# Relative products and causal attention merged into one stage

## The reference

```
q = layernorm(x) @ Wq + bq ;  k = ctx @ Wk + bk ;  v = ctx @ Wv + bv       # per head: [512, 16]
QEr[i, r] = q[i] . Er[r]                                                   # Er: [512, 16]
Srel      = skew(QEr)               # Srel[i, j] = QEr[i, 511 - (i - j)] for j <= i
attn      = softmax((q k^T + Srel) / sqrt(16), causal)
out       = attn @ v
```

## Time and profile before

| | |
|---|---|
| median of three runs | 6249.43 us (6245.49 to 6275.58) |
| span of the profiled execution | 6247.0 us |
| instructions in it | 101,680 |
| PE, DVE, ACT, POOL busy over the span | 74%, 63%, 46%, 33% |
| mean granted TensorE clock | 0.858 of full speed |

### The profile page before, as it was taken

One profiled execution on the slowest core, in us unless ns is written; L12 is line 12 of the kernel. 1 busy time (PEld: TensorE's weight loads), 2 busy tenths in 40 slices (PEclk: granted clock), 3 DMA queues, 4 the chain that ended last, 5 costly groups with the idle time before them and its releaser, 6 DMA issues. The chain is left out here.

```text
span 6247.0 us, 101680 instructions
## 1 busy us (share of the span) xinstructions
PE 4641.5 (74%) x24902; PEld 2868.6 (46%) x24902; DVE 3907.9 (63%) x8145; ACT 2867.3 (46%) x6151; POOL 2042.9 (33%) x3122
## 2 busy tenths in 40 slices
PE   7455666493879973998676767797677887995897
PEld 4113333342643331885234645686555663333433
DVE  6344555538547875443678956558866556886565
ACT  2235655215227753223564556435456323773353
POOL 0113443000036630221443554124542214542342
PEclk9558989696988986999778989998889998997897
DMA  4999986100063321111551232002321115332533
GB/s 158 283 360 190 211 197 157 45 0 0 0 201 89 97 63 45 43 43 41 155 144 62 102 115 65 27 13 92 129 73 41 28 49 182 92 85 82 179 117 100
DMA packets 317791, 648.30 MB, mean 104 GB/s; under 512 B 73170, under 2 KB 128115, under 8 KB 317384
## 3 DMA queue, kind: packets, MB, share of 16 engines
q1 hardware_dynamic: 245912, 450.68, 22.7%
q0 software_dynamic: 71488, 193.32, 13.1%
HBM read 373.99 MB, written 238.70 MB: 98 GB/s over the span
## 5 line engine op out<-in xcount | busy, mean ns | idle before, releaser
L1115 DVE TENSOR_REDUCE t_nmax<-t_aps 128x2 f32<-128x1024 f32 x700 | 838.0, 1221 | 278.2 <-PE t_aps L1037 272.6
L1222 ACT ACTIVATE t_expT<-t_bps 128x512 f32<-128x512 f32 x1290 | 700.9, 599 | 284.4 <-PE t_bps L1056 235.4
L1056 PE MATMUL t_bps<-t_Q,t_K 51*128 51x512 f32 (+2 forms) x1290 | 525.9, 468 | 60.8 <-ACT t_expT L1222 43.8
L1037 PE MATMUL t_aps<-t_K,t_Q 49*128 49x512 f32 (+2 forms) x1400 | 464.7, 460 | 64.7 <-DMA t_K<-k_halves 28.9
L1056 PEld LDWEIGHTS t_bps<-t_Q,t_K 51*128 51x128 f32 (+2 forms) x1290 | 228.8, 189 | 528.6 <-ACT t_expT L1222 373.5
L2517 DVE TENSOR_TENSOR f_hl<-f_h,f_hh 128x512 fp32r<-128x512 f32 x192 | 203.7, 1061 | 413.3 <-ACT f_hh L2442 413.3
L1083 PE MATMUL t_ops<-t_expT,t_V 128*17 128x512 f32 (+1 forms) x2560 | 414.2, 614 | 0.5 <-ACT t_expT L1222 0.4
L3923 ACT ACTIVATE t_relsb<-t_relsb,t_nmax 128x128 f32<-128x128 f32 (+3 forms) x515 | 277.6, 559 | 272.8 <-DVE t_nmax L3896 264.0
L3857 PE MATMUL t_tps<-ident,t_relsb 128*128 128x128 f32 x1280 | 246.6, 296 | 160.1 <-ACT t_expT L3745 149.3
L2806 POOL TENSOR_TENSOR a_crossed<-a_qsb,a_tab 128x256 f32<-128x256 f32 x272 | 268.1, 1007 | 295.9 <-ACT a_qsb L2753 271.3
L1156 POOL DMA_DIRECT2D t_Q<-q_halves x525 | 270.9, 518 | 143.9 <-POOLq L78 72.9
(11 more groups left out here) (441 smaller groups left out, 12543.1 us busy)
## 6 DMA issues: line engine op xcount, KB each, us to landing
rel<-r_out SPq DMA_DIRECT2D x128, 640.0 KB, 5.4
t_relsb<-rel SPq DMA_DIRECT2D x128, 640.0 KB, 5.6
t_Q<-q_halves POOLq DMA_DIRECT2D x420, 64.0 KB, 2.5
t_K<-k_halves POOLq DMA_DIRECT2D x420, 64.0 KB, 2.5
k_halves<-a_parts SPq DMA_DIRECT2D x48, 512.0 KB
q_halves<-a_parts SPq DMA_DIRECT2D x48, 512.0 KB, 5.6
o_xT<-attended SPq DMA_DIRECT2D x32, 512.0 KB, 4.3
f_R<-combine SPq DMA_DIRECT2D x128, 128.0 KB, 3.0
```

What stands on the lines that cost most here:

```text
L1037: last = nc.tensor.matmul(aps[:, (t * PPG + i) % 2, x, :], operand(Qr, KA, p, h, slice(t * P, (t + 1) * P)), operand(Kr, KA, p, h, slice(0 ...
L1056: nc.tensor.matmul(bps[:, slot_of(kb, j), :], operand(Kr, KB, p, h, slice(kb * P, (kb + 1) * P)), operand(Qr, KB, p, h, slice(0, S)), star ...
L1115: nc.vector.tensor_reduce(nmax[:, g, t, i * HPT:(i + 1) * HPT], aps[:, (t * PPG + i) % 2], AX.X, ALU.max, negate=True).then_inc(s["maxed"], 1)
L1222: nc.scalar.activation(expT[:, kb % RING, j, :], bps[:, slot_of(kb, j), :], ACT.Exp).then_inc(s["expo"], 1 + (PAD if end else 0))
```

## The change

`rel_scores` and `causal_attention` are replaced by one phase, `relative_attention`. Its steps are those of the attention, and in each step, behind `scores` and `turn`, PE makes one relative product of a unit six heads ahead (`AHEAD = 6`), for the blocks in the order 3, 1, 0, 2, into two PSUM banks. DVE copies those of blocks 3 and 0, ACT those of 1 and 2, at the end of their steps (`keep_rows`), into one of three `rows` buffers. SP stores the head (`spill`), and behind the store of head n loads head n - 2 skewed (`skew`), into one of five `relsb` buffers. Scores have three PSUM banks in place of four, and `ops` one in place of two. POOL adds the mask with four instructions a head, one for each diagonal block, where three stood. The whole phase is written out without loops or empty instructions.

`qkv` now stores the terms themselves: 96 rows for each head, in six DMAs for each job, twice the bytes. Queries and keys of a batch are loaded in four DMAs of 96 rows x 4 heads each, from POOL's queue, and the queries only once. An unused function `attention` is deleted.

```diff
-                        sp.dma_start(dst.rearrange("r f t -> f r t")[row:row + P, :, ds(b * S, S)],
-                                     parts[:, j % 2]).then_inc(s[f"parts_st{j % 2}"], 16)
+                        h = row // 16
+                        for i, term in enumerate(TERMS):
+                            part = term[dst is not qdst] - 1
+                            sp.dma_start(dst[h:h + P // 16, i * 16:(i + 1) * 16, ds(b * S, S)], parts[:, j % 2, part]).then_inc(s[f"parts_st{j % 2}"], 16)
...
-                        dve.wait_ge(s[f"parts_st{j % 2}"], b * (16 * k) + 16 * (j // 2) + 16)
+                        dve.wait_ge(s[f"parts_st{j % 2}"], b * (ST * k) + ST * (j // 2) + 16)
...
-def rel_scores(nc, G, name, qs, er, rel):
...
-def causal_attention(nc, G, name, qs, ks, vs, rel, odst, sums):
+def relative_attention(nc, G, name, qs, ks, vs, er, rel, odst, sums):
...
     SCORES, EXPO = 4, 3
-    FROM = 3
+    AHEAD = 6
+    SB, RS, RING = 3, 3, 5
+    ORDER = (3, 1, 0, 2)
...
+        def keep_rows(eng, op, n, i, what):
+
+            t = ORDER[i]
+            wait(eng, f"st{n % RS}", 16 * (n // RS))
+            eng.wait_ge(s["product"], n * NT + i + 1)
+            op(rows[:, n % RS, OFF[t]:OFF[t] + WIDTH[t]], rps[:, i % 2, 0:WIDTH[t]]).then_inc(s[what], 1)
...
+                def spill(n):
+                    if n >= NH:
+                        return
+                    sp.wait_ge(s["kept_d"], n * 2 + 2)
+                    sp.wait_ge(s["kept_a"], n * 2 + 2)
+                    sp.dma_start(rel[n:n + 1, :].rearrange("o (p c) -> (o p) c", c=RW), rows[:, n % RS, :]).then_inc(s[f"st{n % RS}"], 16)
+
+                def skew(n):
+                    if not 0 <= n < NH:
+                        return
+                    sp.wait_ge(s[f"st{n % RS}"], 16 * (n // RS + 1))
+                    wait(sp, "turned", (n - RING + 1) * NT)
+                    x = rel[n:n + 1, P - 1:]
+                    sp.dma_start(relsb[:, n % RING, :], bass.AP(x.tensor, x.offset, [[RW - 1, P], [1, RW]])).then_inc(s[f"rel{n % RING}"], 16)
...
+                sp.dma_start(er32, er).then_inc(s["er"], 16)
+                for n in range(NH + 2):
+                    spill(n)
+                    skew(n - 2)
+                    m = n - AHEAD
+                    if m % HG == 0 and m >= 3 * HG:
+                        save(m // HG - 3)
...
+                def load(b, r):
+                    p = b % 2
+                    if r < 2 * QH:
+                        dst, src, what = ((Q, qs, "q"), (K, ks, "k"))[r // QH]
+                        h = r % QH * (H // QH)
+                        pool.dma_start(dst[:, p, h:h + H // QH, :], src.rearrange("h r t -> r h t")[:, h:h + H // QH, b * S:(b + 1) * S]).then_inc(s[f"{what}{p}"], 16)
...
+                def relative(u):
+                    n, i = unit(u)
+                    if n is None:
+                        return
+                    b, h = divmod(n, H)
+                    t = ORDER[i]
+                    if h == 0 and i == 0:
+                        pe.wait_ge(s[f"q{b % 2}"], 16 * QH * (b // 2 + 1))
+                    wait(pe, "kept_a" if i % 2 else "kept_d", n * 2 + i // 2)
+                    nc.tensor.matmul(rps[:, i % 2, 0:WIDTH[t]], Q[:, b % 2, h, t * P:(t + 1) * P], erk[:, S - WIDTH[t]:S],
+                                     start=True, stop=True).then_inc(s["product"], 1)
...
+                def step(u):
+                    scores(u + SCORES)
+                    turn(u)
+                    relative(u + AHEAD * NT)
+                    n, t = unit(u)
+                    if n is not None and t == 1 and n >= HG:
+                        values(n // HG - 1, n % HG)
...
+                def step(u):
+                    least(u + EXPO)
+                    n, t = unit(u)
+                    if n is not None and t % 2 == 0:
+                        copied(dve, nc.vector.tensor_copy, n, t, "cp_dve")
+                    m, i = unit(u + AHEAD * NT - 1)
+                    if m is not None and i % 2 == 0:
+                        keep_rows(dve, nc.vector.tensor_copy, m, i, "kept_d")
+                    if n is not None and t == NT - 1 and n % HG == HG - 1 and n >= 2 * HG - 1:
+                        keep(n // HG - 1)
...
-        G.qs = dram("q_parts", [3, 512, TOK], BF16)
-        G.ks = dram("k_parts", [3, 512, TOK], BF16)
+        qs = dram("q_terms", [16, 96, TOK], BF16)
+        ks = dram("k_terms", [16, 96, TOK], BF16)
...
-            rel_scores(nc, G, "r0", qs, a["L0_xattn_Er"], rel)
-            causal_attention(nc, G, "t0", qs, ks, G.vs, rel, G.osT, G.sums)
+            relative_attention(nc, G, "t0", qs, ks, G.vs, a["L0_xattn_Er"], rel, G.osT, G.sums)
```

More of the change, by code:

```diff
@@ L3715, in walk @@
[L3715 to L3728 removed]
+        rps = ps("rps", [P, 2, S])
@@ L3766, in batch @@
-                def batch(b, first):
-                    for g in range(NG):
-                        for j in range(HG):
-                            load(b, g * HG + j)
-                            if j == 0 and not (first and g < 3):
-                                k = b * NG + g - 3
-                                if g == 3:
-                                    save(k, b, 0)
-                                else:
-                                    save(k, b - 1, g + 1)
-                batch(0, True)
@@ L3892, in least @@
                 def least(u):
-                    if u.t == 0:
-                        wait(dve, "masked", u.head + 1)
-                    wait(dve, "score", u.n + 1)
-                    nc.vector.tensor_tensor_reduce(out=u.tile(), in0=sps[:, u.t, 0:u.w], in1=u.tile(), scale=1.0, scalar=3.0e38,
-                                                   op0=ALU.add, op1=ALU.min, accum_out=nmax[:, u.j, u.t:u.t + 1]).then_inc(s["least"], 1)
-                def keep(g, par, it, i):
-                    wait(dve, "pv", g + 1)
-                    wait(dve, f"o_st{par}", i * (32 * HG))
-                    nc.vector.tensor_copy(osb[:, par, :], ops[:, par, :]).then_inc(s["o_free"], 1)
@@ L3928, in _, with step @@
-                walk(act, step)
+                def step(u):
+                    n, t = unit(u + EXPO)
+                    if n is not None:
+                        act.wait_ge(s["least"], u + EXPO + 1)
+                        nc.scalar.activation(tile(n, t), tile(n, t), ACT.Exp, scale=-1.0, bias=nmax[:, n % RING, t:t + 1]).then_inc(s["expo"], 1)
+                    n, t = unit(u)
+                    if n is not None and t % 2:
+                        copied(act, nc.scalar.copy, n, t, "cp_act")
+                    m, i = unit(u + AHEAD * NT - 1)
+                    if m is not None and i % 2:
+                        keep_rows(act, nc.scalar.copy, m, i, "kept_a")
```

623 lines of the change are left out of this document (123 added, 500 removed).

## The result

The changed kernel takes 6056.61 us (median of four runs, 6046.45 to 6060.27) against 6255.79 for the one before in the same comparisons: a ratio of 0.968, 95% interval 0.9655 to 0.9704, 3.2% faster. The forecast was 6077. The profiled execution has a span of 6055.7 us. Two executions further down took far longer than the others of their kernel (12425 us in `with_nops`, 7994 us of the kernel before in the same comparisons) and are left out of every figure here.

A forecast was written before the change was run, and what follows sets the result against it. The prediction took rel_scores as bound by its stores and the attention by a loop of dependencies. Merging saves 192 us, the projection adds 20: 6247.0 - 172 + 2.4 = 6077 us, range 5970 to 6165.

The forecast's parts named there:

- its own case: Merged attention: the forecast itself, a period of 5.0 to 5.6 us a head, 6035 to 6120 us, chance 0.49.
- the sum: Prologue and attention 719 us against 911, 192 us less; the projection adds 20; total -172 us.
- signs of being wrong: PE products waiting for stores, DVE for POOL at each head's first block, or a projection ending after 210 us.
- no stretch at a DMA share of 1 with idle engines: Sign of being right: none such between 190 and 450 us.
- What goes: From rel_scores' first instruction to the attention's first score product, 333.4 us; only a prologue of 29 us replaces it.
- The steady loop: Attention: the loop now runs through ACT's 384-wide copy and PE's 256-wide relative product; period 4.38 + 0.9, say 5.3 us.
- The added piece: Attention's loop: exponential 0.6, copy 0.45 and product 0.2, less 0.37 for turn of block 1: 0.9 us a head.
- The base of that loop: The old attention's period of 4.38 us a head, carried over into the merged stage.
- The projection: qkv: six stores of 768 KB a job instead of one of 384 KB, +20 us over eight batches, bounds 0 and 60.
- The transfers: Stores, skewed loads, results and terms in the merged stage: 4.55 to 5.7 us a head, taken as 4.8, below the loop.
- The rival in which they bind: Transfers become the bound of the merged stage: period 5.7 to 6.0 us, 6127 to 6162 us, chance 0.21.
- Slower than before: Merged stage: the skewed load lands too late, above 13.3 us; at 16 us the kernel takes 6394 us; chance 0.05.

The follow-up runs named there:

- with_nops: The changed kernel with empty instructions put back behind the waits of PE, DVE and ACT and some of SP and POOL in the merged stage; 6123.92 us, ratio 0.9787.
- old_no_nops: The kernel before, without the empty instructions behind the waits of TensorE and ScalarE in its attention; 6235.85 us against 6252.25, ratio 0.9976.
- flat_terms: The changed kernel, but the projection's six stores of a job write 128 neighbouring DRAM rows instead of 8 heads x 16 rows; 6031.62 us, ratio 0.9623.
- values_first: The changed kernel, but in each step PE does its part of values before the relative product; 6029.27 us, ratio 0.9617.
- interleaved: The changed kernel with the 96 rows of a head ordered feature by feature, the six terms inside; 6020.84 us, ratio 0.9623.

## Why the prediction was right

Its direction, its loop and its range held, the period of 5.11 us lies in its own case (5.0 to 5.6), and the total came out 20 us from the measured time. That closeness is in part luck. The stage after its start came out 40 us below the sum and the projection 35 above it, and these cancel; 14 of the 20 us that are left lie behind the last copy, in work that the change does not touch. One of the prediction's own signs of being wrong also came true: the projection ended after 210 us (221.6). And the sign "no stretch at a DMA share of 1 with idle engines" failed from 230 to 300 us.

- **What goes.** 333.4 us became 24.5 (forecast 29). The first relative product came 11.5 us after the stage's start (14).
- **The steady loop.** The loop was the one forecast: the order of time shows each of its steps, half the bytes leave the period at 4.93, and moving `values` past the waiting product shortens it. The added piece was forecast at 0.9 us. It measures 0.88 by the shortest intervals (4.88 less 4.00) and 1.11 on the mean of the full intervals (5.11 less 4.00); the difference holds the dips of the clock, for which the sum had no term.
- **The base of that loop** is the first mis-sized term. I took the old 4.38 us over and wrote that the dropped empty instructions "could still contribute a little". In the merged stage the base is 4.00, against 4.51 for the old stage by the same measure. In the terms of the sum it is 0.38 lower than the 4.38 taken over, 46 us over 122 heads; the addition is 0.21 higher than forecast, 26 us; and the last six heads and the ends took 31 us where the sum had 43. Together these are about the 35 us by which this piece came out lower. With the empty instructions put back the merged stage takes 5.32 us a head, close to the 5.28 of the sum, but that is no proof: in the old kernel those of PE and ACT were worth 0.11 us, and the products themselves bring new waits, each with its own empty instruction. What makes up the rest of the 0.51 stays open. The trace of before did hold a sign: the earlier trace rows has 243 instructions of DVE in the written-out slice and 229 in the looped one, which I read as no gain and which is 6% more work done; the six full intervals of the written-out batches average 4.26 us a head, the 22 later ones 4.57. That this is due to the loops isn't shown either, since in `old_no_nops` the two parts take 4.49 and 4.37.
- **The projection** is the second. Forecast +20 us, measured +54.5. The sum assumed issues of 0.37 us and stores on all engines; with such stores (flat_terms) the term measures +12.8. The rest, 41.7 us, comes from the shape of the DRAM side: the 8 engines, and the issue of 0.62 us, which the same edit takes away. The sentence on the Trainium skill's rule put this at 12 us more than I took, in all 32; its direction was right and its size too small, perhaps because the issue too rose, which no run separates. I should have given that rule a chance of its own.
- **The transfers** were placed between 4.55 and 5.7 us a head and taken as 4.8, under the loop. That they stay under the loop was right for the changed kernel; the 4.8 was too high, since with `values` first the full intervals average 4.73, and with the earlier load 4.56. The rival in which they bind is what happens one step later.
- **Slower than before** needed a skewed load that lands in 13.3 us. The median was 6.6 us, and DVE waited for POOL 41 us in 605.
- **The end.** The unchanged stages behind the last copy took 5168.6 us before, 5154.8 after, and between 5151 and 5178 in the other profiled executions, with no relation to the edit that I can name. The 14 us between before and after therefore say nothing about the change. This scatter, up to 27 us, is also why a stage's gain of 46 us (values_first) came out as 27 in the medians (39 by the two ratios to the kernel before). The same 21186 products keep PE busy 3945 us where this part is short (after) and 3984 where it is long (interleaved), so the granted clock differs there; what makes it differ is left open.

## What to carry to other kernels

Merging two stages pays where one is bound by transfers and the other by a loop of waits; the work that is added is free only where it is not in front of an instruction of that loop, so look at what stands behind each new wait in its engine's order. A new DRAM layout is to be checked on both its sides: one that makes loads wide can make stores narrow, and here one reordering of rows gave both. Empty instructions between waits belong in the sum of a loop of waits, even if they are never busy; they also hide in a profile whom the next instruction waited for. A period is best read from intervals of the same work, and its shortest and its mean interval tell apart the loop itself and what disturbs it.

## What the runs showed of the hardware

A store from SP whose DRAM side began with a dimension of 8 ended with 8 small packets fewer than one with 128 rows at one pitch, took SP 0.61 to 0.62 us instead of 0.33 to 0.40 to issue, and cost the projection 42 us. The kernel with an empty instruction behind each wait took 0.40 us a head more in a loop of about 5 us, 0.20 of it in turns that nothing disturbs. In the same merged stage the cut to half the bytes was worth nothing with one order of instructions on PE and 0.49 us a head with another. For the same work of PE over the full intervals (2910 to 2913 instructions) the granted clock was 0.86 with the empty instructions, 0.91 in the changed kernel, and 1.00 with `values` first and half the bytes; where it fell to 0.50, a part of `values` took 1.91 us instead of 1.05.
